# A graph-attention kernel on one core: first input and last chain in halves, attention columns and three spreads by TensorE, outer orders rewritten

## The reference, cut to what matters

```python
h = relu(layernorm(x))
# graph attention with 4 heads, then one more over their concatenation
Wh = einsum('bnf,hfo->bhno', h, W_heads)
f1 = Wh @ a[:, :O];  f2 = Wh @ a[:, O:]
e = leaky_relu(f1[..., None] + f2[:, :, None, :], 0.01)
e = where(adj > 0, e, -1e9)
h = elu(softmax(e) @ Wh)            # heads concatenated: 1024 features
out = elu(gat(h, W_out, a_out))     # one head, 256 features
y = relu(out @ w1 + b1) @ w2 + b2 + out
x = x + layernorm(y) * gamma + beta
# graph convolution
h = relu(layernorm(x))
x = x + deg * (h @ Wi.T + b) + adj @ (h @ Wj.T)
```

## Time and profile before

| what | value |
|---|---|
| median of 3 runs | 1374.18 us (1373.8 to 1378.77) |
| the profiled execution | 1378.36 us, its span 1376.6 us |
| PE busy | 1299.2 us, 94% of the span |
| DVE busy | 1100.5 us, 80% |
| ACT busy | 1113.1 us, 81% |
| POOL busy | 370.1 us, 27% |
| mean granted clock of PE | 0.979 |

### The profile page before, as it was taken

How to read it: one execution, slowest core, us unless ns; L and a number is a source line. 1 busy time by engine, 2 the same in 40 slices (tenths; PEclk the granted TensorE clock), 3 DMA queues, 4 the chain that set the end, 5 groups by cost and what they waited for, 6 DMA issues and landing times.

```text
span 1376.6 us, 27572 instructions
## 1 busy us (share of the span) xinstructions
PE 1299.2 (94%) x10024; PEld 1248.1 (91%) x10024; DVE 1100.5 (80%) x2874; ACT 1113.1 (81%) x2144; POOL 370.1 (27%) x247
## 2 busy tenths in 40 slices
PE   4699999999999999999999999999999999998864
PEld 4599999999999999999999999999999999998753
DVE  7977789788888979888887978888897888877542
ACT  4788988898887988888898888889898888878431
POOL 0021331423233141322315132322314232331411
PEclk9799999999999999999999999999999999999986
DMA  6201001011110111011010101111010110101000
GB/s 214 85 17 37 19 16 48 24 46 41 40 47 17 47 31 49 30 40 48 16 57 22 55 24 39 47 32 54 17 50 22 48 39 24 48 16 40 8 31 16
DMA packets 42743, 55.16 MB, mean 40 GB/s; under 512 B 2864, under 2 KB 30832, under 8 KB 42480
## 3 DMA queue, kind: packets, MB, share of 16 engines
q1 hardware_dynamic: 42608, 53.39, 12.6%
HBM read 44.83 MB, written 8.55 MB: 39 GB/s over the span
## 4 chain that ended last, share of the span: by engine, by line
PE 86%; ACT 5%; DVE 5%; issue 2%; DMA 1%; POOL 0%; SPq 0%; ACTq 0%; DVEq 0%
PE ps L1018 66%; PE ps L1086 9%; PE ps L1183 4%; PE ps L1149 4%; PE ps L1124 1%; PE ps L1158 1%; PE ps L1048 1%; ACT arg L710 1%; DVE arg L905 1%; DVE prob_lo L882 1%; ACT prob_hi L716 1%; PE ps L1077 1%; ACT arg L706 1%; ACT elu L731 1%; DMA f2bc<-f_rows 0%
## 5 line engine op out<-in xcount | busy, mean ns | idle before, releaser
L598 POOL TENSOR_TENSOR hx_lo<-elu,hx_hi 128x512 fp32r<-128x512 f32 x128 | 168.2, 1314 | 693.3 <-ACT hx_hi L740 691.9
L1018 PE MATMUL ps<-prob_hi,whx_hi 128*128 128x256 f32 x1024 | 296.2, 289 | 4.0 <-DVE prob_lo L882 3.1
L1018 PE MATMUL ps<-prob_hi,whx_lo 128*128 128x256 f32 x1024 | 290.3, 283 | 0.0
L1018 PE MATMUL ps<-prob_lo,whx_hi 128*128 128x256 f32 x1024 | 290.2, 283 | 0.0
L710 ACT ACTIVATE arg<-arg,nmax 128x512 f32<-128x512 f32 x320 | 227.0, 713 | 4.6 <-DVE nmax L916 4.4
L905 DVE CUSTOM_DVE_ANT_0 arg<-f2bc,mask 128x512 f32<-128x512 f32 x320 | 220.9, 728 | 4.3 <-PE ps L1086 2.9
L706 ACT ACTIVATE arg<-arg,fcol 128x512 f32<-128x512 f32 x320 | 212.5, 715 | 9.1 <-DVE gmax L905 8.9
L882 DVE TENSOR_TENSOR prob_lo<-ps,prob_hi 128x1024 fp32r<-128x1024 f32 x160 | 195.1, 1219 | 28.4 <-ACT prob_hi L716 28.3
L1018 PEld LDWEIGHTS ps<-prob_hi,whx_hi 128*128 128x128 f32 x1024 | 196.3, 192 | 7.6 <-DVE prob_lo L882 4.2
L1018 PEld LDWEIGHTS ps<-prob_hi,whx_lo 128*128 128x128 f32 x1024 | 196.7, 192 | 0.2
L1018 PEld LDWEIGHTS ps<-prob_lo,whx_hi 128*128 128x128 f32 x1024 | 196.5, 192 | 0.0
(11 more groups left out here) (129 smaller groups left out, 3243.7 us busy)
## 6 DMA issues: line engine op xcount, KB each, us to landing
f2bc<-f_rows SPq DMA_DIRECT2D x80, 256.0 KB, 3.3
xin<-in_x SPq DMA_DIRECT2D x16, 512.0 KB, 4.0
xb<-in_x SPq DMA_DIRECT2D x16, 512.0 KB, 4.9
out_x<-xb SPq DMA_DIRECT2D x16, 512.0 KB, 2.9
f_rows<-f2row SPq DMA_DIRECT2D x80, 2.0 KB
ff<-in_L_gnn_a_heads SPq DMA_DIRECT2D x1, 1024.0 KB, 7.8
arg<-in_adj SPq DMA_DIRECT2D x1, 1024.0 KB, 10.0
ff<-in_L_gnn_W_out SPq DMA_DIRECT2D x1, 1024.0 KB, 5.4
```

The costliest lines, as they stand in the source:

```text
L598: pool.tensor_tensor(out=hx[1][:, 2 * c.h:2 * c.h + 2, c.u * HN:(c.u + 1) * HN], in0=elu[:, c.buf, :, :], in1=hx[0][:, 2 * c.h:2 * c.h + 2 ...
L1018: i = pe.matmul(out, a, b_, start=(k == 0), stop=(k == n - 1))
```

## The change

Four things change.

1. Halves. x of batch 0 is loaded in two transfers, and norm_in, norm_in_out and turn_in of batch 0 run as two steps of two row tiles each (the second is written `norm_in:1@0`). For the last batch the same holds for turn_out, ffn1, ffn2, norm_ff, norm_ff_out, gamma, x2, norm_gc, norm_gc_out, bias, turn_gc, conv and store. Both halves of a PE step share one PSUM pair. m1:00 and conv_in:0 wait for the first half alone.
2. The f columns of W_heads by PE. a_heads is loaded as 16 rows of 128 (8 KB) and turned (a_turn), W_heads is turned by 16 transposes (wh_turn:0, :1) and copied by ACT, and wsum makes all columns with 16 accumulation pairs; DVE's wh_sum rounds them. wh_prep on DVE is gone.
3. Three spreads by PE. For heads 0 and 1 of batch 0 and the last attention of batch 15, f2pe multiplies the row by a selecting matrix of ones, so that the spread f2 lies in PSUM, and rowmax reads it there. f2send and f2bcast of these do nothing.
4. The mask loses a cast (the comparison reads the integers). FIRST and LAST are new on all engines; ROUND is as before.

```diff
+            def wh_turn(c):                      # PE
+                pe.wait_ge(ld[LD_WH], 16 * KC)
+                for h in range(H):
+                    for o in range(KC):
+                        q = KC * h + o
+                        i = pe.transpose(pairs[c.pair][:, q // 4, q % 4 * P:(q % 4 + 1) * P], w_heads[k][:, h, o * P:(o + 1) * P], ident[:, :])
+            def wsum(c):                         # PE
+                pe.wait_ge(s_whT, KC)
+                pe.wait_ge(s_aT, 1)
+                for k in range(KC):
+                    for h in range(H):
+                        for o in range(KC):
+                            col = 2 * (H * k + h)
+                            i = pe.matmul(pairs[c.pair][:, 0, col:col + 2], wT[:, k, KC * h + o, :],
+                                          aT.rearrange("p (h s o) -> p h o s", h=H, s=2)[:, h, o, :], start=(o == 0), stop=(o == KC - 1))
+            def f2pe(c):                         # PE
+                pe.wait_ge(f2_row, head + 1)
+                for n in range(NC):
+                    i = pe.matmul(pairs[c.pair][:, 0, n * P:(n + 1) * P], ident[0:NC, n:n + 1].to_broadcast([NC, P]), f2row[:, :],
+                                  start=True, stop=True)
+                lend((c.pair,), (max_made, 4 * (head + 1)))
+            def wh_sum(c):                       # DVE
+                dve.wait_ge(s_wsum, 1)
+                for k in range(KC):
+                    i = dve.tensor_copy(wh[0][:, k, :, F:FA], cols[:, k, :, :])
+                link(i)
+                for k in range(KC):
+                    i = dve.tensor_tensor(out=wh[1][:, k, :, F:FA], in0=cols[:, k, :, :], in1=wh[0][:, k, :, F:FA].bitcast(fp32), op=ALU.subtract)
-                    for z in range(2):
-                        i = dot(w_heads[k][:, h, :], a_h[:, h, z, :], wsum[:, k, h, z:z + 1], 2 * k + z)
-                link(dve.tensor_copy(adj_m[:, tiles, :], adj_m[:, tiles, :].bitcast(i32)))
-                dve.tensor_scalar(mask[:, tiles, :], adj_m[:, tiles, :], 0.0, BIG, ALU.is_gt, ALU.mult).then_inc(s_edges, 1)
+                dve.tensor_scalar(mask[:, tiles, :], adj_m[:, tiles, :].bitcast(i32), 0.0, BIG, ALU.is_gt, ALU.mult).then_inc(s_edges, 1)
...
-            sp.dma_start(xin[:, :, :], x_v[0]).then_inc(x_loaded, 16)
+            sp.dma_start(xin[:, 0:2, :], x_v[0][:, 0:2, :]).then_inc(x_half, 16)
+            sp.dma_start(xin[:, 2:NC, :], x_v[0][:, 2:NC, :]).then_inc(x_loaded, 16)
-                         a_heads.partition_broadcast(P)).then_inc(ld[LD_A], 16)
+            sp.dma_start(a_rows, a_heads.rearrange("h (z q) -> (h z) q", q=P)).then_inc(ld[LD_A], 16)
```

The new orders, at the places that the prediction speaks of:

```diff
 PE, start
-    turn_in@0 m1:00@0 m1:01@0 m1:10@0 m1:11@0 f2turn:0@0 gc_turn@0 m1:20@0 m1:21@0 m1:30@0 f2turn:1@0 f2turn:2@0 m1:31@0
+    wh_turn:0@0 wh_turn:1@0 a_turn@0 turn_in@0 wsum@0 turn_in:1@0 gc_turn@0 m1:00@0 m1:01@0 m1:10@0 f2turn:0@0 f2pe:0@0
+    m1:11@0 m1:20@0 f2turn:1@0 m1:21@0 f2pe:1@0 m1:30@0 turn_p:0@0 turn_in@1 f2turn:2@0 m1:31@0 attend:0@0 turn_p:1@0
 DVE, start
-    norm_in@0 norm_in_out@0 wh_low:0@0 wh_low:1@0 wh_prep:0@0 wh_prep:1@0 turn_in@0 mask:0@0 wh_prep:2@0 wh_low:2@0 m1:00@0
+    norm_in@0 norm_in:1@0 norm_in_out@0 norm_in_out:1@0 mask:0@0 mask:1@0 wh_low:0@0 wh_low:1@0 turn_in@0 wh_low:2@0 wh_sum@0
+    mask_end:0@0 wh_low:3@0 turn_in:1@0 mask_end:1@0 m1:00@0 gc_turn@0 m1:01@0 norm_in@1 m1:10@0 rowmax:0@0 norm_in_out@1
 PE, end
-    attend:8@-1 attend:9@-1 mix2:0@-1 mix2:1@-1 mix2:2@-1 mix2:3@-1 turn_gc@-2 f2turn:-1@-1 conv_in:0@-2 conv_in:1@-2 conv@-2
-    turn_p:4@-1 turn_p:5@-1 attend:4@-1 attend:5@-1 turn_out@-1 ffn1@-1 ffn2@-1 turn_gc@-1 conv_in:0@-1 conv_in:1@-1 conv@-1
+    turn_p:9@-1 attend:8@-1 attend:9@-1 mix2:0@-1 mix2:1@-1 mix2:2@-1 turn_gc@-2 mix2:3@-1 conv_in:0@-2 conv_in:1@-2
+    f2turn:-1@-1 f2pe:-1@-1 conv@-2 turn_p:4@-1 turn_p:5@-1 attend:4@-1 attend:5@-1 turn_out@-1 turn_out:1@-1 ffn1@-1
+    ffn1:1@-1 ffn2@-1 ffn2:1@-1 turn_gc@-1 turn_gc:1@-1 conv_in:0@-1 conv_in:1@-1 conv@-1 conv:1@-1
 POOL, end
-    x_beta@-2 hx_lo:7@-1 norm_ff@-2 hx_lo:8@-1 gamma@-2 hx_lo:9@-1 norm_gc@-2 bias@-2 x_beta@-1 add_b2@-1 norm_ff@-1 gamma@-1
-    norm_gc@-1 bias@-1
+    norm_ff@-2 hx_lo:6@-1 gamma@-2 hx_lo:7@-1 hx_lo:8@-1 hx_lo:9@-1 norm_gc@-2 bias@-2 x_beta@-1 add_b2@-1 norm_ff@-1
+    norm_ff:1@-1 gamma@-1 gamma:1@-1 norm_gc@-1 norm_gc:1@-1 bias@-1 bias:1@-1
```

More of the change, by code:

```diff
@@ L18 @@
[L18 to L22, removed]
@@ L27 @@
+    conv_in:0@0 f2turn:3@2 conv_in:1@0 turn_p:4@1 attend:3@2 m1:10@3 turn_p:5@1 attend:4@1 turn_p:6@2 m1:11@3 attend:5@1
+    f2turn:0@3 conv@0 turn_out@1 attend:6@2 turn_p:7@2 turn_p:8@2 ffn1@1 attend:7@2 f2turn:1@3 attend:8@2 m1:20@3 turn_p:9@2
+    m1:21@3 ffn2@1 m1:30@3 attend:9@2 turn_p:0@3 mix2:0@2 mix2:1@2 turn_p:1@3 mix2:2@2 mix2:3@2 attend:0@3 m1:31@3 f2turn:-1@2
+    turn_in@4 attend:1@3
     """,
     "ACT": """
-    wh_prep:0@0 wh_prep:1@0 norm_in_out@0 turn_in@0 w1_prep@0 m1:00@0 wh_prep:2@0 wh_prep:3@0 mask:0@0 m1:01@0 m1:10@0 m1:11@0
@@ L109 @@
+    store@-4 load_back@-3 f2send:1@-1 f2bcast:1@-1 f2send:-1@-2 f2bcast:-1@-2 f2send:2@-1 f2bcast:2@-1 store@-3 load_back@-2
+    f2send:3@-1 f2bcast:3@-1 f2send:-1@-1 f2bcast:-1@-1 store@-2 load_back@-1 store@-1 store:1@-1
     """,
     "PE": """
-    f2turn:2@-5 turn_p:2@-5 m1:00@-4 turn_gc@-7 turn_p:3@-5 m1:01@-4 attend:2@-5 conv_in:0@-7 f2turn:3@-5 conv_in:1@-7
-    turn_p:4@-6 attend:3@-5 turn_p:5@-6 m1:10@-4 attend:4@-6 m1:11@-4 attend:5@-6 turn_p:6@-5 conv@-7 turn_out@-6 f2turn:0@-4
-    attend:6@-5 turn_p:7@-5 ffn1@-6 turn_p:8@-5 attend:7@-5 f2turn:1@-4 turn_p:9@-5 attend:8@-5 m1:20@-4 ffn2@-6 m1:21@-4
@@ new lines @@
+    attend:8@-4 ffn2@-5 turn_p:0@-3 attend:9@-4 m1:21@-3 mix2:0@-4 mix2:1@-4 m1:30@-3 turn_p:1@-3 mix2:2@-4 mix2:3@-4
+    attend:0@-3 m1:31@-3 turn_in@-2 f2turn:-1@-4 attend:1@-3 turn_p:2@-3 f2turn:2@-3 turn_gc@-5 turn_p:3@-3 m1:00@-2
+    f2turn:3@-3 m1:01@-2 attend:2@-3 conv_in:0@-5 turn_p:4@-4 attend:3@-3 attend:4@-4 turn_p:5@-4 conv_in:1@-5 m1:10@-2
+    attend:5@-4 f2turn:0@-2 conv@-5 turn_p:6@-3 turn_p:7@-3 turn_out@-4 m1:11@-2 attend:6@-3 ffn1@-4 turn_p:8@-3 attend:7@-3
+    f2turn:1@-2 m1:20@-2 attend:8@-3 turn_p:9@-3 ffn2@-4 turn_p:0@-2 m1:21@-2 attend:9@-3 mix2:0@-3 attend:0@-2 m1:30@-2
@@ L447, in gnn_kernel @@
                       "elu_out", "hx", "hx_lo")
-        IN_PSUM = ("turn_in", "m1", "f2turn", "turn_p", "attend", "mix2", "turn_out", "ffn1", "ffn2", "turn_gc", "conv_in", "conv", "gc_turn", "adj_turn")
+        IN_PSUM = ("turn_in", "m1", "f2turn", "turn_p", "attend", "mix2", "turn_out", "ffn1", "ffn2", "turn_gc", "conv_in", "conv", "gc_turn", "adj_turn",
+                   "wh_turn", "a_turn", "wsum", "f2pe")
         def parse(text):
```

620 lines of the change are left out of this document (348 added, 272 removed).

## The result

| | kernel before | changed kernel |
|---|---|---|
| median | 1374.39 us (1373.8 to 1378.77, 5 runs) | 1365.61 us (1363.56 to 1367.21, 5 runs) |
| profiled execution | 1378.36, span 1376.6 | 1367.08, span 1365.3 |

The ratio is 0.9919, 95% interval 0.9903 to 0.9935: the changed kernel is faster by 0.8%: 8.8 us between the medians, 9 to 13 us by the interval. Forecast were 23.5 us, 1351 us, and the range from 1343 to 1361 does not hold the time.

The account below looks back on a forecast made before the run. PE was taken to bound 160 to 1200 us, leaving only the ends: a DVE queue in the head, a serial string in the tail. Gains 7 + 1.5 + 15 = 23.5 us gave 1351 us, range 1343 to 1361.

Parts of the forecast that it names:

- the two ends: Head and tail of the span: only these can give time, since PE is busy 1039.65 of 1040 us between.
- the string in halves: Last attend's end to span's end, 55.4 us before: 39.0 to 42.0 in halves, gain 15 us, bounds 10 and 18.
- I take a gain of 1.5, the wait removed, and let the other two cancel; bounds -2 and 4: Middle of the tail: PE's wait before conv_in:0 goes; the later f2turn:-1 and other moves cancel.
- Rival 5: New LAST order over five batches: a step too early stalls PE in each batch; slower, 1382 us; chance 0.05.
- The announced sign: PE waits between 160 and 1200 us would show the forecast wrong; right was a steady stretch 99.9% PE.
- the last spread: Tail: f2turn:-1 stands behind both conv_in steps; conv covers rowmax, args and scale with 1 to 2 us missing.
- the price of wsum: Head: 16 narrow products on PE ahead of the first m1, bounds 1.1 to 3.9 us.
- I charge 1 us: Head: first m1 starts 0.5 to 4.5 us later; 1 us charged, as DVE has other work meanwhile.
- the relief behind the first m1: Head: 7.9 us less DVE work, 1.2 for the wait on the first f2bc, less 1 for new waits.
- Rival 2: Head gives nothing, as ACT sets the pace from 160 back to 60 us: 1358 us; chance 0.12.
- Rival 1: Slow PE clock at both ends: head loses 2 us more, tail 1.5: 1354 us; chance 0.15.
- Head: Start of the kernel: less DVE work and a removed wait, minus later start and new waits; 7 us, bounds 0 and 11.

Follow-up runs that it names:

- r2: The changed kernel run again, unchanged, in a later set: 1366.98 us, ratio 0.9923 to the kernel before.
- e2: The changed kernel with the old order of the last part and a whole end, its last spread by DMA; only the new head left: 1372.09 us, ratio 0.9960.
- e3: The changed kernel with its new order of the last part, but a whole end and the last spread by DMA: 1384.32 us, ratio 1.0049.
- e5: The changed kernel with the products of wsum done twice: 1371.34 us, ratio 0.9963.
- e6: The changed kernel with 16 products of the identity on PE before the first weights land: 1361.69 us, ratio 0.9887.
- e10: The changed kernel with f2 of batch 0's heads 0 and 1 spread by DMA as before, w1_low moved behind rowmath:0: 1370.27 us, ratio 0.9951.
- r1: The changed kernel run again, unchanged, beside follow-up runs: 1365.31 us, ratio 0.9908 to the kernel before.

## Why the prediction was wrong

**The reading of the whole was right**: only the two ends could give time, and the string in halves was priced well. Forecast 39.0 to 42.0 us, measured 40.3, 40.1 and 39.1; the gain taken was 15 against 15.2. Some of that is luck. Two errors cancelled in it: in r2, where ffn1 runs at the full pace that the sum begins with, conv_in starts at 23.1, not 21.4, and takes 7.1 us, not 8.4. Against the whole end behind the new head (53.4 and 53.7 in e2 and e3) the halves give 13.1 to 14.6.

**The step that failed first: "I take a gain of 1.5, the wait removed, and let the other two cancel; bounds -2 and 4".** The body lost 7.0. The wait of 1.49 us in front of conv_in did go; the rest of the rewritten order, which the sum put at nothing, cost 8.5. I read only the few steps around mix2:3@-1, while LAST covers five batches. Rival 5 had the mechanism, a step too early on an in-order engine, but its price was set per batch and its chance, 0.05 "with all lesser stalls", was far too small: an order that leaves PE idle for 0.35 us in 1040 can only be kept or made worse, and a new one has to match it at every step. The announced sign, waits of PE between 160 and 1200, came as described. For the last spread I had the trade right way round, f2turn:-1 late and the PE spread making up for it, but took it for even: the late f2turn:-1 costs 7.6 us and the spread gives 5.6 back (e3 against e2 and the changed kernel).

**The second: the price of wsum and "I charge 1 us" for the later first m1.** The bounds for the narrow products were 1.1 to 3.9 us, built from transposes. Measured are 6.96 at the slow pace and 3.7 to 3.9 at the full one. A product of two columns is not cheap here: each is two instructions, and each of these loads 128 columns of fp32 weights, which fills the time (6.9 us of loading in 6.96). The weights' arrival was taken as 7.67 us as well, and was 8.3 to 9.9. The Trainium skill says that a true fp32 product takes four passes (FP8 and Floating Point Precision, TensorE Precision Notes) and that loading weights takes time by their columns, columns / 1.2 ns (TensorE: Matmul & The Clock Gate, LDWEIGHTS); the estimate from both is 16 x 4 x 0.107 = 6.8 us. The slow pace, 6.96, agrees with it; the full pace does not, with 3.7 to 3.9. I had read neither for this. The first m1 came at 19.3 to 24.0 in the three profiles of the changed kernel, forecast 16 to 20, and e5 and e6 show that this passes on one for one. Charging 1 us for up to 4.5 rested on DVE's other work; in e5 none of it stood in for m1.

**In the other direction: the relief behind the first m1 is larger, not smaller.** Forecast 7.9 + 1.2 - 1 = 8.1; measured 774.1 less 763.2 to 763.8, 10.3 to 10.9. The gain seems to sit elsewhere than I put it: e10 gives some 6.6 to 7.0 us for the two spreads together with w1_low's place, where I had booked 1.2 for the spread. That would leave some 4 for the DVE work of 7.9, if the two add up, which no run shows. The first turn_p came at 41.3 in the first profile and at 37.3 in r1, against 38 forecast; the first rowmax at 31.1 and 27.1, for the 28 named. Rival 2 (ACT takes the whole lead back) is refuted, but part of it is lost: at ACT's first read of an attend (50.9 against 55.9 us) the lead is 5.0 us and at the 18th (171.4 against 174.5) 3.1; in r1 9.0 and 7.1. Rival 1, the slow pace, came true in the head in two of the three profiles (m1 at 23.0 and 24.0, against 19.3), and in the last ffn1 in two as well (4.57 us in the first and in r1, 3.11 in r2).

**The sum.** Head +7 forecast, +3.1, +7.1 and +1.8 in three profiles of the changed kernel; middle +1.5, measured -7.0; string +15, measured +15.2. So of the 12.2 us missing in the profiled executions (23.5 less 11.3), 8.5 are the order of the last part and 3.9 the head. In the median 8.8 us were gained; the profiled execution of the kernel before was 4 us slower than its median, that of the changed kernel 1.5 us.
